# Second layer of a two-layer convolution kernel: two block buffers, a scratch tensor stored row by row, one load for each block

## The chip, the core and the metric

## What is computed

The input x is 8 images of 32 channels of 512 x 512 in float32. Cut to what matters:

```python
# layer 0
x = x + _L0_conv_ref(_gn(x), L0_conv_weight, L0_conv_bias)   # 3x3 convolution of quantised values
# layer 1, on x1 = the x above
v = _gn(x)                                    # groups of 2 channels: (v - mean) / sqrt(var + eps)
feat = einsum('bihw,oi->bohw', v, conv_w) + conv_b
filt = einsum('kh,bchw,lw->bckl', Ph, feat, Pw)   # 5x5 means of feat: a filter for each image and channel
out = x + depthwise 5x5 convolution of feat with filt
```

## The kernel before

Three stages run one after the other: the first layer, a short stage that makes statistics and filter tables, and the second layer.

**First layer** (`quantised_conv`). A chunk is 32 image rows (16 chunks an image). Its SBUF tile `b_x` has row r of each group of 4 in partitions 32r to 32r+31, a channel in each partition, 8 groups side by side; a chunk is loaded by four DMAs of 32 partitions (L321). Part of the next image is streamed through `b_stream` (L355) for its statistics. After the convolution the sum stands in the same tile, and GpSimd stores it to the scratch tensor x1 in HBM (L561), four DMAs of 32 partitions, 2 KB pieces. x1 has the layout image, channel, row, column. SyncE reloads a slot only when its store has landed.

**Second layer** (`depthwise`). An image is 9 blocks of 57 output rows (61 input rows); 72 blocks. Each block goes through 8 steps s, with 4 channels of the output in each step. A group(p, e, j) works on two blocks at once: the pointwise part of block j and the banded part (the 5x5 filter as matmuls with banded tables) of block j-1.

- `c_x` holds one block of x1 in float32, partitions being (column quarter, channel), 61 rows of 128 columns, so rows of 512 B. It has one buffer. Four DMAs load it (L832): SyncE those of quarters 0 and 1, ScalarE those of 2 and 3, both at step 2 of the group before, when VectorE's last c_z of the old block is done (`zl_done`).
- ScalarE writes the high half of a part of the block (a quarter of its columns) to `c_z` (L942), VectorE the low half (L971). Parts 0 and 1 of block j+1 come in steps 6 and 7 of group j, parts 2 and 3 in steps 0 and 1 of the next group.
- TensorE multiplies 8 column positions of `c_z` a step into `c_cps` (24 matmuls, L1032 to L1034). ScalarE takes the result to `c_feat` high (L959), VectorE to `c_feat` low (L997).
- TensorE multiplies the banded tables `c_tt` with `c_feat` into `c_tps` (36 matmuls a step, L1052). Both PSUM tiles have two slots.
- `c_xr` holds x1 for the same output rows, 4 channels a step, 6 slots (half a 128-partition tile each). SyncE loads it (L844): rows 0 to 47 and 48 to 56 in a DMA each, once the slot's old content is stored (`stored`). VectorE adds `c_tps` to it (L1007, two instructions a step), and GpSimd stores it to the output (L911).

SyncE executes one program in order: the c_xr of each step, at step 2 of each group the wait for `zl_done` and its half of c_x, and towards the end of an image the tables. This loop runs from registers (`Fori` over pairs of images). A DMA that stands behind another on the same queue is issued after it.

## Time and profile before

| | us |
|---|---|
| median of 3 runs | 7573.3 (7562.2 to 7585.8) |
| the profiled execution, own time | 7568.0 |
| its span | 7566.2 |
| first layer, about | 0 to 2780 |
| second layer, about | 2930 to 7566 |

The profile is of one execution. Busy time is the time in which an engine ran instructions; matmuls are pipelined, so TensorE's is rough. A wait names the instruction or transfer that came last before the waiting one could go. A wait matters only if the engine that waits, or one that waits for it, sets the pace. Lines such as L1007 are lines of the kernel before. Transfers into SBUF are named by tile: c_x<-x_scratch is a load of the block, c_xr<-x_scratch one of the rows to be added to.

### The profile page before, as it was taken

What the parts mean: (1) busy time and instruction counts of PE and PEld (TensorE: products, weight loads), DVE (VectorE), ACT (ScalarE), POOL (GpSimd) and SP (SyncE); (2) the same over time, 40 slices, a digit from 0 to 9 for tenths busy, and PEclk for the clock granted to TensorE, in tenths of its full rate; (3) what the DMA queues carried; (4) which work ended last, traced back from release to release, by engine and by line L of the source; (5) the groups of instructions that cost most, each with busy time, mean ns of one, the idle gap of its engine ahead of it and who ended that gap; (6) DMA issues with size and microseconds to landing.
All of it is one profiled execution on the core that took longest, in us unless ns stands there. A gap on an engine that the chain in (4) does not pass through costs nothing.

```text
span 7566.2 us, 113303 instructions
## 1 busy us (share of the span) xinstructions
PE 5144.7 (68%) x43798; PEld 3402.5 (45%) x43798; DVE 5236.3 (69%) x5651; ACT 3292.3 (44%) x1645; POOL 995.8 (13%) x1700
## 2 busy tenths in 40 slices
PE   0766666666666753776777776777777677777677
PEld 0111111111111213665666665666666566666566
DVE  4676767777676873666777776766666677677676
ACT  0655546455554743333443343443333343444343
POOL 0011101011010111111111111111111111111111
PEclk9888878877888876888888888888888888888888
DMA  9999999999999866777778778778877877877877
GB/s 199 263 257 285 262 284 261 270 281 272 281 263 290 255 182 137 184 181 193 182 184 198 177 190 197 185 181 204 188 181 187 197 188 177 202 182 179 193 185 184
DMA packets 1136887, 1615.31 MB, mean 213 GB/s; under 512 B 84538, under 2 KB 642874, under 8 KB 1132346
## 3 DMA queue, kind: packets, MB, share of 16 engines
q1 hardware_dynamic: 689154, 928.05, 52.8%
q0 software_dynamic: 166336, 537.04, 24.1%
q10 hardware_dynamic: 280832, 142.62, 8.3%
q8 instruction: 363, 5.95, 0.3%
q14 instruction: 202, 1.65, 0.1%
HBM read 1068.53 MB, written 538.84 MB: 212 GB/s over the span
## 4 chain that ended last, share of the span: by engine, by line
DMA 21%; DVE 14%; PE 9%; issue 8%; SPq 7%; ACT 3%; another core or an unknown queue 1%; POOL 0%; ACTq 0%; DVEq 0%; POOLq 0%
DMA c_x<-x_scratch 12%; DMA c_xr<-x_scratch 9%; PE c_tps L1052 8%; DVE c_z L971 7%; SPq L844 5%; DVE c_xr L1007 5%; DVE c_feat L997 2%; ACT c_z L942 2%; SPq L832 1%; ACT c_feat L959 1%; PE c_cps L1032 0%; PE c_cps L1034 0%; PE c_cps L1033 0%; SPq L849 0%
## 5 line engine op out<-in xcount | busy, mean ns | idle before, releaser
L1052 PE MATMUL c_tps<-c_feat,c_tt 123*128 123x256 f16 (+1 forms) x20736 | 2660.2, 292 | 1183.8 <-DVE c_xr L1007 923.9
L1052 PEld LDWEIGHTS c_tps<-c_feat,c_tt 123*128 123x128 f16 (+1 forms) x20736 | 2130.7, 104 | 1603.3 <-DVE c_xr L1007 878.3
L1007 DVE SCALAR_TENSOR_TENSOR c_xr<-c_tps,c_xr 57x1024 f32<-57x1024 f32 (+1 forms) x1152 | 1403.7, 1218 | 1225.7 <-DMA c_xr<-x_scratch 1114.9
L942 ACT ACTIVATE c_z<-c_x,c_rs 128x1952 f16<-128x1952 f32 x288 | 1062.4, 3690 | 1418.9 <-DMA c_x<-x_scratch 1320.3
L428 PE MATMUL b_ps<-b_xq,w0main 128*128 128x512 bf16 x3072 | 954.1, 416 | 808.5 <-ACT b_q L390 671.5
L959 ACT ACTIVATE c_feat<-c_cps 122x1024 f16<-122x1024 f32 x576 | 818.6, 1423 | 1492.5 <-PE c_cps L1034 1239.0
L911 POOL DMA_DIRECT2D out_dram<-c_xr x1152 | 666.8, 580 | 4040.1 <-DVE c_xr L1007 3962.9
L971 DVE SCALAR_TENSOR_TENSOR c_z<-c_x,c_rs,c_z 128x1952 f16<-128x1952 f32 x288 | 1030.8, 3579 | 195.0 <-ACT c_z L942 192.0
L390 ACT ACTIVATE b_q<-b_ps,q_bias 128x1024 int8<-128x1024 f32 x512 | 549.9, 1113 | 1031.9 <-DVE b_x L506 965.1
L1032 PE MATMUL c_cps<-w_high,c_z 128*128 128x128 f16 x4608 | 813.9, 221 | 190.6 <-DVE c_z L971 122.3
L441 PE MATMUL b_ps<-b_xq,w0edge 64*32 64x512 bf16 x3048 | 926.9, 415 | 0.0
L438 PE MATMUL b_ps<-b_xq,w0edge 64*32 64x512 bf16 x3048 | 925.2, 414 | 0.0
L428 PEld LDWEIGHTS b_ps<-b_xq,w0main 128*128 128x128 bf16 x3072 | 226.0, 101 | 1485.6 <-issue 1232.8
L997 DVE TENSOR_TENSOR c_feat<-c_cps,c_feat 122x1024 f16<-122x1024 f32 x576 | 813.6, 1413 | 71.2 <-ACT c_feat L959 54.0
L465 DVE BATCH_NORM_STATS2 b_stats_x<-b_stream 128x6 f32<-128x512 f32 x672 | 413.9, 680 | 584.4 <-DMA b_stream<-in_x_dram 538.7
L1034 PE MATMUL c_cps<-w_high,c_z 128*128 128x128 f16 x4608 | 812.0, 221 | 0.0
L1033 PE MATMUL c_cps<-w_low,c_z 128*128 128x128 f16 x4608 | 811.7, 220 | 0.0
L517 DVE BATCH_NORM_STATS2 b_stats<-b_x 128x6 f32<-128x408 f32 (+5 forms) x1520 | 645.4, 501 | 4.0
L561 POOL DMA_DIRECT2D x_scratch<-b_x x512 | 298.9, 584 | 2449.6 <-DVE b_cols L521 2248.4
L506 DVE SCALAR_TENSOR_TENSOR b_x<-b_q,b_x 128x2048 f32<-128x2048 int8 x256 | 574.6, 2280 | 60.2 <-ACT b_q L390 60.2
L1032 PEld LDWEIGHTS c_cps<-w_high,c_z 128*128 128x128 f16 x4608 | 454.1, 99 | 203.3 <-DVE c_z L971 116.0
L375 ACT ACTIVATE b_x<-b_x,b_shift,b_scale 128x4096 int8<-128x4096 f32 x128 | 486.7, 3802 | 42.1 <-DVE b_shift L476 40.6
(130 smaller groups left out, 2283.4 us busy)
## 6 DMA issues: line engine op xcount, KB each, us to landing
b_x<-in_x_dram SPq DMA_DIRECT2D x552, 512.0 KB, 15.3
x_scratch<-b_x POOLq DMA_DIRECT2D x512, 512.0 KB, 10.8
c_xr<-x_scratch SPq DMA_DIRECT2D x576, 384.0 KB
out_dram<-c_xr POOLq DMA_DIRECT2D x576, 384.0 KB, 5.1
b_stream<-in_x_dram SPq DMA_DIRECT2D x672, 256.0 KB, 12.9
c_x<-x_scratch SPq DMA_DIRECT2D x112, 976.0 KB, 17.4
c_x<-x_scratch ACTq DMA_DIRECT2D x112, 976.0 KB, 20.9
c_tt<-table_scratch SPq DMA_DIRECT2D x64, 576.0 KB
```

Source lines behind the costliest of these rows:

```text
L428: return pe.matmul(ps[:, g % 3, j, :], k.w0main[:, d, :, :].rearrange("p r o -> p (r o)"), xq[:, n % XQ_SLOTS, 2 * i + j, d:d + W], start= ...
L438: pe.matmul(ps[0:C, g % 3, j, :], k.w0edge[P // 2:P, d, :], xq[P // 2:P, (m - 1) // JB % XQ_SLOTS, (m - 1) % JB, d:d + W], start=False, st ...
L441: pe.matmul(ps[P - C:P, g % 3, j, :], k.w0edge[0:P // 2, d, :], xq[0:P // 2, (m + 1) // JB % XQ_SLOTS, (m + 1) % JB, d:d + W], start=False ...
L942: act.activation(split_part(0, part), positions(part), ACT.Identity, scale=rs[:, :]).then_inc(zh_done, 1)
L959: act.activation(dst, cps[0:MAIN, s % 2, :, :].rearrange("p j (q o) -> p o q j", q=Q), ACT.Identity).then_inc(fh_done, 1)
L971: dve.scalar_tensor_tensor(split_part(1, part), positions(part), rs[:, :], split_part(0, part), ALU.mult, ALU.subtract).then_inc(zl_done, 1)
L997: dve.tensor_tensor(lo, cps[0:MAIN, s % 2, :, :].rearrange("p j (q o) -> p o q j", q=Q), hi, ALU.subtract).then_inc(fl_done, 1)
L1007: last = dve.scalar_tensor_tensor(res, tps[PR * h:PR * h + n, s % 2, :, :], 1.0 / FS, res, ALU.mult, ALU.add)
L1032: pe.matmul(dst, zh, wh, start=True, stop=False)
L1033: pe.matmul(dst, zh, wl, start=False, stop=False)
L1034: last = pe.matmul(dst, zl, wh, start=False, stop=True)
L1052: last = pe.matmul(tps[:, s % 2, o % 4, :], tt[0:rows, o, tp, 2 * d:2 * d + 2, :].rearrange("k w m -> k (w m)"), feat[0:rows, (e * N + i) ...
```

## The change

What it does:

1. x1 is laid out image, row, channel, column. The store from `b_x` is two DMAs of all 128 partitions (4 of the 8 groups each) where it was four of 32. The partitions of `c_x` become (channel, column quarter), and a block is loaded by one DMA over 128 partitions, issued by SyncE; ScalarE issues none. The weight tile `w1_diag` is filled by four small strided loads, and `rstd` is copied to the new partition order (`rstd_cq`).
2. `c_x` gets two buffers. The load of block j+2 is issued at step 5 of group j, when all of block j is split.
3. The parts of a block are split in every second step, two steps ahead of their use; `c_z` holds two parts and no longer a whole block. The order on VectorE is feat, c_z, addition.
4. `c_xr` has 4 slots for 6. Its four channels of a row stand together in HBM, so a row is one run of 8 KB for four of 2 KB.
5. SyncE's program of the second layer is written out for all 72 blocks, with constants for register values.
6. Constants of the first layer are freed before the second, to make room.

The diff, cut to its core:

```diff
-XR_SLOTS = 6
+XR_SLOTS = 4
...
-        x1v = x1.rearrange("b c (n j r) w -> b n r c j w", j=JB, r=4)
+        x1v = x1.rearrange("b (n j r) c w -> b n (r c) j w", j=JB, r=4)
+        STORE = 2 * 16
...
-                    for r in range(Q):
-                        pool.dma_start(x1v[b, n, r, :, :, :], xt[C * r:C * r + C, s, :, :]).then_inc(x1_stored[s], 16)
+                    for h in range(2):
+                        rows = slice(JB // 2 * h, JB // 2 * (h + 1))
+                        pool.dma_start(x1v[b, n, :, rows, :], xt[:, s, rows, :]).then_inc(x1_stored[s], 16)
...
+            for q in range(Q):
+                sp.dma_start(rstd_cq[q::Q, :], rstd[0:C, :]).then_inc(stored, 16)
...
-        xt = sb("c_x", [P, ROWS_IN, P], F32)
-        z = sb("c_z", [P, 2, W // Q // 2, P], F16)
+        xt = sb("c_x", [P, 2, ROWS_IN, P], F32)
+        z = sb("c_z", [P, 2, 2, PAIRS_PART, P], F16)
...
-        x1v = x1.rearrange("b c h (q w) -> b q c h w", q=Q)
+        x1v = x1.rearrange("b h c (q w) -> b (c q) h w", q=Q)
...
-        def load_x1(eng, p, e, j, quarters):
-
-            if (e, j) != (0, 0):
-                eng.wait_ge(zl_done, count(p, e, 4 * N, 4 * j) + START)
+        def load_x1(eng, p, e, j):
+
+            if (e, j) not in ((0, 0), (0, 1)):
+                eng.wait_ge(zl_done, count(p, e, 4 * N, 4 * (j - 1)) + START)
...
-            for q in quarters:
-                eng.dma_start(xt[C * q:C * q + C, lo:hi, :], x1v[e + de::2][p, q, :, r0 + lo:r0 + hi, :]).then_inc(x1_loaded, 16)
+            eng.dma_start(xt[:, x_slot(e, j), lo:hi, :],
+                          x1v[2 * p + e + de, :, r0 + lo:r0 + hi, :]).then_inc(x1_loaded[x_slot(e, j)], 16)
...
-                    if s == 2 and pointwise and (j < N - 1 or another(p, e)):
-                        load_x1(sp, p, e, j + 1, (0, 1))
+                    if s == 5 and pointwise and (j + 2 < N or another(p, e)):
+                        load_x1(sp, p, e, j + 2)
...
-            run(sp, group)
+            group(0, 0, 0, True, False)
+            for p in range(PAIRS):
+                for e in range(2):
+                    for j in range(1, N + 1):
+                        group(p, e, j, p < PAIRS - 1 or e == 0 or j < N, True)
...
-        def convert_order(p, e, j, s):
-
-            if 1 <= j and s < 2:
-                return [(j, 2 + s)]
-            if s >= STEPS - 2 and (j + 1 < N or another(p, e)):
-                return [(j + 1, s - (STEPS - 2))]
-            return []
+        def convert_next(p, e, j, s):
+
+            if s % 2:
+                return None
+            if s < STEPS - 2:
+                return j, s // 2 + 1
+            return (j + 1, 0) if j + 1 < N or another(p, e) else None
...
-                    if s == 2 and (j < N - 1 or another(p, e)):
-                        load_x1(act, p, e, j + 1, (2, 3))
...
-    x1 = nc.dram_tensor("x1_scratch", [nb, C, H, W], F32).ap()
+    x1 = nc.dram_tensor("x1_scratch", [nb, H, C, W], F32).ap()
```

Two places in the program. First SyncE in the middle of a block of the second layer, before: each c_xr is two DMAs (48 and 9 rows), ISA and REGISTER_ALU rows compute addresses, and the two c_x rows are SyncE's half of a block; the c_xr before them is that of step 2.

```order
L844 ISA [waits c_stored4]
L844 DMA c_xr<-x_scratch 48x4x512
L844 ISA
L844 DMA c_xr<-x_scratch 9x4x512
L827 REGISTER_ALU
L832 ISA [waits c_zl_done]
L832 DMA c_x<-x_scratch 32x61x128
L832 ISA
L832 DMA c_x<-x_scratch 32x61x128
L844 ISA [waits c_stored5]
L844 DMA c_xr<-x_scratch 48x4x512
```

The same engine after, in the second group of the image: the c_xr rows shown first are those of steps 4 and 5.

```order
L860 DMA c_xr<-x_scratch 48x2048 [waits c_stored0]
L860 DMA c_xr<-x_scratch 9x2048
L860 DMA c_xr<-x_scratch 48x2048 [waits c_stored1]
L860 DMA c_xr<-x_scratch 9x2048
L847 DMA c_x<-x_scratch 128x61x128 [waits c_zl_done]
L860 DMA c_xr<-x_scratch 48x2048 [waits c_stored2]
L860 DMA c_xr<-x_scratch 9x2048
L860 DMA c_xr<-x_scratch 48x2048 [waits c_stored3]
L860 DMA c_xr<-x_scratch 9x2048
```

The load of the block moved from behind the c_xr of step 2 to behind that of step 5, and it is one DMA of 128 partitions where SyncE had two of 32; the c_xr of steps 6 and 7 stand behind it.

Second VectorE, before, in steps 1 and 2 of a group: c_z is the low half of a part, c_feat the low half of feat, c_xr the addition.

```order
L971 SCALAR_TENSOR_TENSOR c_z<-c_x,c_rs,c_z 128x16x122 [waits c_zh_done]
L994 REGISTER_ALU
L997 TENSOR_TENSOR c_feat<-c_cps,c_feat 122x32x4x8 [waits c_fh_done]
L1007 SCALAR_TENSOR_TENSOR c_xr<-c_tps,c_xr 57x1024 [waits c_xr_loaded3,c_band_done]
L1007 SCALAR_TENSOR_TENSOR c_xr<-c_tps,c_xr 57x1024
L994 REGISTER_ALU
L997 TENSOR_TENSOR c_feat<-c_cps,c_feat 122x32x4x8 [waits c_fh_done]
L1007 SCALAR_TENSOR_TENSOR c_xr<-c_tps,c_xr 57x1024 [waits c_xr_loaded4,c_band_done]
L1007 SCALAR_TENSOR_TENSOR c_xr<-c_tps,c_xr 57x1024
```

And after, one even step and the odd one behind it.

```order
L1016 TENSOR_TENSOR c_feat<-c_cps,c_feat 122x32x4x8 [waits c_fh_done]
L992 REGISTER_ALU
L993 SCALAR_TENSOR_TENSOR c_z<-c_x,c_rs,c_z 128x16x122 [waits c_zh_done]
L1024 REGISTER_ALU
L1029 SCALAR_TENSOR_TENSOR c_xr<-c_tps,c_xr 57x1024 [waits c_xr_loaded2,c_band_done]
L1029 SCALAR_TENSOR_TENSOR c_xr<-c_tps,c_xr 57x1024
L1013 REGISTER_ALU
L1016 TENSOR_TENSOR c_feat<-c_cps,c_feat 122x32x4x8 [waits c_fh_done]
L1024 REGISTER_ALU
L1029 SCALAR_TENSOR_TENSOR c_xr<-c_tps,c_xr 57x1024 [waits c_xr_loaded3,c_band_done]
```

c_z went behind feat, and comes in every second step all through the group where it stood at the head of steps 6, 7, 0 and 1 in a row.

## Rows read from the trace of the kernel before

**Rows 1.** Stretches: length; busy (instructions) by engine; granted clock, DMA share, GB/s

```profile
20.00:170.00 150.00, 0.00 (x0) 0.00 (x0) 72.66 (x120) 0.00 (x0) 0.38 (x1) 1.00 1.07 219
300.00:2700.00 2400.00, 1619.32 (x8437) 418.31 (x8436) 1763.25 (x2994) 1340.14 (x711) 275.48 (x472) 0.82 1.00 274
2930.00:7566.00 4636.00, 3374.84 (x34481) 2936.37 (x34478) 3193.76 (x2032) 1809.41 (x858) 666.83 (x1152) 0.85 0.79 187
```

**Rows 2.** Waits, second layer: us in total, times, longest

```profile
ACT c_z L942 <- DMA c_x<-x_scratch: 1196.8, 70, 23.5
DVE c_xr L1007 <- DMA c_xr<-x_scratch: 1114.9, 78, 18.8
PE c_tps L1052 <- DVE c_xr L1007: 923.9, 91, 15.6
PE c_tps L1052 <- DVE c_feat L997: 259.8, 64, 5.9
...
DVE c_z L971 <- ACT c_z L942: 137.1, 47, 14.2
DVE c_xr L1007 <- PE c_tps L1052: 98.7, 81, 2.0
...
DVE c_feat L997 <- ACT c_feat L959: 54.0, 26, 8.5
```

**Rows 3.** Groups of instructions, second layer: busy us, mean ns, idle before

```profile
L1007 DVE SCALAR_TENSOR_TENSOR c_xr<-c_tps,c_xr 57x1024 f32<-57x1024 f32 (+1 forms) x1152 | 1403.7, 1218 | 1225.7 <-DMA c_xr<-x_scratch 1114.9 <-PE c_tps L1052 98.7
...
L971 DVE SCALAR_TENSOR_TENSOR c_z<-c_x,c_rs,c_z 128x1952 f16<-128x1952 f32 x284 | 1016.7, 3580 | 140.1 <-ACT c_z L942 137.1
...
L997 DVE TENSOR_TENSOR c_feat<-c_cps,c_feat 122x1024 f16<-122x1024 f32 x574 | 810.9, 1413 | 71.2 <-ACT c_feat L959 54.0
```

**Rows 4.** Timeline of SyncE's queue, one block: start us, us, what

```profile
5106.31 1.60 SPq L832 DMA_DIRECT2D c_x<-x_scratch  x2
5108.09 38.33 SPq L844 DMA_DIRECT2D c_xr<-x_scratch  x16
```

**Rows 5.** What SyncE's queue waited for, second layer

```profile
SPq L832 <- DVE c_z L971: 1655.6, 70, 44.0
```

**Rows 6.** The chain that ended last, same block: start us, us, what

```profile
5108.09 9.99 SPq L844
...
5118.26 12.07 DMA c_xr<-x_scratch
```

**Rows 7.** Timeline of VectorE, same block

```profile
5114.29 1.42 DVE L997 TENSOR_TENSOR c_feat<-c_cps,c_feat 122x1024 f16<-122x1024 f32 x1
5130.43 1.22 DVE L1007 SCALAR_TENSOR_TENSOR c_xr<-c_tps,c_xr 57x1024 f32<-57x1024 f32 x1 [14.71 <-DMA c_xr<-x_scratch]
```

**Rows 8.** Timeline of TensorE, the banded matmuls of three steps after a wait

```profile
5006.46 6.29 PE L1052 MATMUL c_tps<-c_feat,c_tt 123*128 123x256 f16 x36 [12.61 <-DVE c_xr L1007]
...
5013.93 4.11 PE L1052 MATMUL c_tps<-c_feat,c_tt 123*128 123x256 f16 x36
...
5019.22 4.11 PE L1052 MATMUL c_tps<-c_feat,c_tt 123*128 123x256 f16 x36
```

**Rows 9.** DMA queues, 5108 to 5110: packets, MB, share of 16 engines

```profile
q1 hardware_dynamic: 589, 0.30, 72.0%
q10 hardware_dynamic: 30, 0.02, 3.4%
```

**Rows 10.** DMA queues, 2866 to 2870

```profile
q1 hardware_dynamic: 1140, 0.58, 58.3%
q10 hardware_dynamic: 1142, 0.58, 57.5%
```

**Rows 11.** DMA queues, 5117 to 5121

```profile
q0 software_dynamic: 254, 0.67, 42.4%
```

**Rows 12.** DMA queues, 300 to 2700

```profile
q1 hardware_dynamic: 217601, 409.80, 68.9%
q0 software_dynamic: 67408, 245.46, 30.7%
```

**Rows 13.** The output stores of L911, from its own view

```profile
DMA to landing us min/median/max: 2.8/5.7/18.9
```

**Rows 14.** What SyncE's queue waited for, first layer

```profile
SPq L321 <- DMA x_scratch<-b_x: 701.7, 96, 23.0
```

**Rows 15.** Timeline of ScalarE, first block of the second layer

```profile
2855.57 2.55 ACTq L832 DMA_DIRECT2D c_x<-x_scratch  x2
2907.32 3.57 ACT L942 ACTIVATE c_z<-c_x,c_rs 128x1952 f16<-128x1952 f32 x1 [123.59 <-DMA c_x<-x_scratch]
```

More of the change, by code:

```diff
@@ L45 @@
 SPLIT = 48
+PAIRS_PART = 16
 def edges(i):
@@ L600, in _, with filters @@
             dve.wait_ge(kept, 1 + START)
-def filters(nc, nb, k, sums, mean, rstd, table_d, bias_d):
+def filters(nc, nb, k, sums, mean, rstd, rstd_cq, table_d, bias_d):
     lots = -(-nb // 4)
@@ L731, in _ @@
         def _(sp):
+            for q in range(Q):
+                sp.dma_start(rstd_cq[q::Q, :], rstd[0:C, :]).then_inc(stored, 16)
             sp.wait_ge(tables_ready, 1)
@@ L762, in depthwise @@
         xr = sb("c_xr", [P, XR_SLOTS // 2, 4, W], F32)
-        rs = sb("c_rs", [P, 1], F32)
+        rs = sb("c_rs", [P, 2], F32)
         cps = ctx.enter_context(nc.psum_tensor("c_cps", [P, 2, 8, P], F32))
         tps = ctx.enter_context(nc.psum_tensor("c_tps", [P, 2, 4, HW2], F32))
-        x1_loaded, edge_loaded = sem("c_x1_loaded"), sem("c_edge_loaded")
+        x1_loaded = [sem(f"c_x1_loaded{i}") for i in range(2)]
+        edge_loaded = sem("c_edge_loaded")
         t_loaded = [sem(f"c_t_loaded{i}") for i in range(4)]
@@ L947, in group @@
                 if not banded:
-                    load_x1(act, p, e, 0, (2, 3))
-                    for part in range(4):
-                        high(p, e, 0, part)
+                    high(p, e, 0, 0)
                 else:
@@ L954, in group @@
                 for s in range(STEPS):
-                    for blk, part in convert_order(p, e, j, s):
-                        high(p, e, blk, part)
+                    nxt = convert_next(p, e, j, s)
+                    if nxt is not None:
+                        high(p, e, *nxt)
                     act.wait_ge(conv_done, count(p, e, TILES, STEPS * j + s + 1) + START)
@@ L998, in group @@
                                           ALU.subtract).then_inc(fl_done, 1)
+                        nxt = convert_next(p, e, j, s)
+                        if nxt is not None:
+                            low(p, e, *nxt)
                     if banded:
@@ L1011, in _ @@
             for t in range(2):
-                dve.memset(z[:, t, :, MAIN:P], 0.0).then_inc(started, 1)
+                dve.memset(z[:, t, :, :, MAIN:P], 0.0).then_inc(started, 1)
             for slot in range(2):
@@ L1029, in pointwise @@
                 for c in range(8):
-                    zh, zl = (z[:, t, 8 * s + c, :] for t in range(2))
+                    zh, zl = (z[:, s // 2 % 2, t, 8 * (s % 2) + c, :] for t in range(2))
                     dst = cps[:, s % 2, c, :]
@@ L1087, in conv_preact_2 @@
-        k.b1col = sb("b1col", [P, 1], F32)
-        k.below = sb("below", [P, NBINS - 1], F32)
-        k.above = sb("above", [P, NBINS - 1], F32)
-        k.bin_weight = sb("bin_weight", [P, NBINS, NBINS], F32)
-        own = sb("own", [P, nb, 2], F32)
-        mean = sb("mean", [P, nb], F32)
-        rstd = sb("rstd", [P, nb], F32)
-        with ExitStack() as tmp:
-            weights_and_masks(nc, tmp, k, w0, b0, w1, b1)
-        with nc.sbuf_tensor("sums", [P, nb, NSEG, 2 * NBINS - 1], F32) as sums:
-            quantised_conv(nc, nb, k, x, x1, own, sums)
-            statistics_of_x1(nc, nb, k, own, mean, rstd)
-            filters(nc, nb, k, sums, mean, rstd, table_d, bias_d)
@@ L1100, in conv_preact_2, with early @@
-        depthwise(nc, nb, k, x1, rstd, table_d, bias_d, out)
+        rstd_cq = sb("rstd_cq", [P, nb], F32)
+        with ExitStack() as first:
+            def early(name, shape, dt):
+                return first.enter_context(nc.sbuf_tensor(name, shape, dt))
+            k.same_group = early("same_group", [P, P], F32)
+            k.same_channel = early("same_channel", [P, P], F32)
+            k.w0main = early("w0main", [P, 3, Q, C], BF16)
+            k.w0edge = early("w0edge", [P, 3, C], BF16)
+            k.w1t = early("w1t", [P, C], F32)
+            k.wf = early("w1_diag", [P, Q, C], F32)
+            k.b0col = early("b0col", [P, 1], F32)
+            k.q_bias = early("q_bias", [P, 1], F32)
+            k.b1col = early("b1col", [P, 1], F32)
+            k.below = early("below", [P, NBINS - 1], F32)
+            k.above = early("above", [P, NBINS - 1], F32)
+            k.bin_weight = early("bin_weight", [P, NBINS, NBINS], F32)
+            own = early("own", [P, nb, 2], F32)
+            mean = early("mean", [P, nb], F32)
+            rstd = early("rstd", [P, nb], F32)
+            with ExitStack() as tmp:
+                weights_and_masks(nc, tmp, k, w0, b0, w1, b1)
+            with nc.sbuf_tensor("sums", [P, nb, NSEG, 2 * NBINS - 1], F32) as sums:
+                quantised_conv(nc, nb, k, x, x1, own, sums)
+                statistics_of_x1(nc, nb, k, own, mean, rstd)
+                filters(nc, nb, k, sums, mean, rstd, rstd_cq, table_d, bias_d)
@@ L1104 @@
+        depthwise(nc, nb, k, x1, rstd_cq, table_d, bias_d, out)
 _INS = ["x", "L0_conv_weight", "L0_conv_bias", "L1_conv_conv_w", "L1_conv_conv_b"]
```

75 lines of the change are left out of this document (37 added, 38 removed).

## The prediction

> **What bounds the kernel now.** I read the stretches first [rows 1]. The first layer (300 to 2700 us) keeps the DMA engines busy all the time, share 1.00 at 274 GB/s; the second (2930 to 7566, 4636 us) does not, 0.79 at 187 GB/s. The reader is to see there that no engine is full (VectorE 3193.8 us, TensorE 3374.8), so a wait sets the pace. The table of waits says which [rows 2]: VectorE's addition L1007 waits 1114.9 us for the transfers c_xr, 78 times, some 14 us each; for ScalarE's c_z it waits 137.1, for ScalarE's feat 54.0, for TensorE 98.7, while TensorE waits 923.9 and 259.8 for VectorE. ScalarE waits longer for the blocks c_x (1196.8) but has room for it. The second layer is 72 blocks (8 images of 9), so a block takes 4636/72 = 64.4 us. VectorE's work in it, from the mean durations [rows 3]: 16 x 1.218 + 4 x 3.580 + 8 x 1.413 = 45.1 us. The rest is 15.5 of c_xr waits and 3.8 of others.
>
> **Where the c_xr wait is born.** Three engines in one block: SyncE sends its half of c_x at 5106.31, and only then the c_xr of step 3 [rows 4]; it had sat waiting for VectorE's c_z (L832, 1655.6 us in all) though slots were free [rows 5]. The chain shows SyncE held for 9.99 us in that next issue, then 12.07 us to its landing [rows 6]; VectorE had finished feat of step 3 by 5115.7 and goes on at 5130.43 [rows 7]. From the issue of c_x to the addition behind it are L = 24.1 us. Work that VectorE has in hand at that point: two additions and three feats, 9.1 us. So the wait is about 15: that is the pace. The block is L plus the work from that addition to the c_z that releases the next c_x: 2.44 + 2 x 3.85 + 3 x 7.43 + 3.58 = 36.0 (3.85 a step without c_z, 7.43 with one), plus 3.8 of small waits: 63.9, against 64.4 seen.
>
> **The change, part by part.** *SyncE's order.* By the order of the program c_x of block j+2 stands behind the c_xr of step 5, and steps 6 and 7 and the following ones stand behind it. Its wait is for the last c_z of block j, now in step 4. So the loop has the old shape: c_x issued at the end of c_z in step 4, c_xr of step 6 behind it on the same queue. Work in hand: additions of 4 and 5, feats of 5 and 6, c_z of 6, 2.44 x 2 + 1.41 x 2 + 3.58 = 11.3 us. Work after: addition 6 (2.44), steps 7, 1, 3 (11.6), steps 0 and 2 (14.9), feat and c_z of step 4 (5.0), together 33.9. Block time T = L' + 33.9 + small waits. Four slots instead of six matter little for step 7 to step 1 (their slots are free by then); later slots are asked for again after some 7.5 us (POOL's issue 0.6, landing 5 to 6 [rows 13]) of about 20 us of work.
>
> *What the earlier load buys.* c_x is needed a block after its issue, so ScalarE's 1196.8 us of waiting goes, but VectorE had only 137.1/72 = 1.9 us a block of it, and ScalarE no longer issues DMAs (0.75 a block of feat waits). A c_z in every second step evens VectorE's pairs of steps at 11.3 us against TensorE's 2 x 5.3 (from one group of 36 matmuls to the next 5.29); after a stop that group takes 6.29 where it takes 4.11 in full run [rows 8]. I leave 2.1 us of small waits where 3.8 were, bounds 1 and 4. T = L' + 36.0.
>
> *L', the term that decides.* Before, two queues carried the block: 3904 packets of 512 B on SyncE's, 3904 on ScalarE's. Now all 7808 (128 partitions x 61 rows) are on SyncE's. While SyncE's queue was nearly alone it started 589 packets in 2 us, 295 in a us, and its packets took 72% of the engines, so the engines had time left [rows 9]. With both queues in flight, each started 1140 in 4 us, 285 in a us, and the engines were full [rows 10]. A queue alone thus is no faster than a queue beside another. One point speaks for more than 295: SyncE's packets took 0.72 x 32/589 us = 39 ns alone, 33 beside ScalarE's; with the gap of 15 ns kept and 33 ns of packet it would be 333. I take 320, bounds 240 (64 KB from row to row of a partition may be worse than 2 KB) and 592 (both queues' engine limit, 27 ns). So 7808/320 = 24.4 us; out's packets, those of three steps, some 340 of 4 KB at 166 ns [rows 11], take 3.5 us of the engines, of which 3.0 hold it up, the rest falls into its gaps; first packet 1.4 after the issue; then c_xr of step 6 at 8 KB a row: 467 KB at the 219 GB/s of loads that go to half the partitions [rows 1] is 2.1, landing and wake-up 1.5. L' = 32.4, T = 68.4, or 4.0 more than 64.4. Over the 70 blocks that have such a load: +280 us. The place: T = 44.0 + 7808/R, and every 10% of R is about 2.4 us a block, 170 us in all.
>
> The row says one queue gives half of two. The Trainium skill, "DMA: Bandwidth & Descriptors", section "Issuing engines are not separate DMA queues", says that all queues run on the same 16 engines and that a second issuer saves sequencer time only. By that rule R would be that of both queues, 570, and T 57.7; by the row it is about 300. It is the rival C below.
>
> *The store of x1.* Four stores of 32 partitions become two of 128, and a row's 32 channels stand together. The stores took 30.7% of 2400 us for 245.46 MB in 4 KB packets, 197 ns each [rows 12]; where stores ran among loads they took 166 ns (42.4% of 4 us, 0.67 MB) [rows 11]. Loads alone into 32 partitions at a time make 219 GB/s with full engines [rows 1], so a transfer over part of the partitions is slowed by its own kind. If all 65,536 packets fall to 166: 65536 x 31 ns/16 = 127 us, and since the layer's engines are full it would be time won. I take 100, bounds 150 won and 60 lost (SyncE waits 701.7 us for these stores [rows 14], and a slot now needs both of two bigger ones).
>
> On this the skill speaks for the change: "SBUF — State Buffer", section "Door 1: The DMA port swizzle (why `[64,N]` ≈ `[32,N]`)", gives 32 partitions 8 of 16 ports, some 218 GB/s; the 219 GB/s of the load-only stretch agrees.
>
> *At nothing, or nearly.* c_xr at 8 KB a row: 3.65 MB a block in a quarter of the pieces, on a queue that then is idle; only the one behind c_x is in the sum. w1 by four tiny loads and rstd by four, 2 to 3 us once. SyncE's written-out program drops its register steps (37 and 29 ns each), none on the path for more than 0.1 us a block, and adds code to fetch. First block: c_x 0 and 1 now stand before the tables on the queue, about 50 us for both, where before 51.7 us went by from the issue to the first c_z [rows 15]; within 15 us either way.
>
> **The sum**, on the profiled execution's own 7568 us (the median of three is 7573, 5 more): 7568 + 280 - 100 = 7748, say 7750.
>
> **Rivals.**
> A, the forecast: one queue starts 265 to 353 packets a us; T 73.5 to 66.1; 8105 down to 7590.
> B, slower still: the new rows of 64 KB slow each read. R under 265, for instance 240: T 76.5, 7568 + 847 - 100 = 8315. Against it: a block's 64 KB rows are read whole by neighbouring partitions.
> C, faster than before: a single load over all 128 partitions runs at what both queues did. The wait of L1029 then shrinks, since T falls below 64.4 at R above 383, with the store's 100 us counted above 358. At 412: T 63.0, 7370; at 500: 59.6, 7130; at 592: 57.2, 6965. For it: 39 against 33 ns, and engines not full in [rows 9]. Against it: 285 a us beside another queue, where the packets were short too.
> D, the stall doesn't occur: c_xr of step 6 gets past c_x. Then VectorE's 45.1 and 2 of small waits bind, unless the DMA engines do, 0.79 x 64.4 = 50.9 us of work now; 7568 - 70 x 13.5 - 100 = 6523. Against it: [rows 6], where nothing passed.
> E, no change: R of 353 to 363, within 0.3% (what a measurement of this kernel can tell from nothing).
>
> **Chances.** A 0.42, B 0.13, C 0.36, D 0.03, E 0.06. Slower by over 0.3%: A and B, 0.55; within 0.3% 0.06; faster 0.39. The range leaves out the ends of C with D (below 7150, some 0.11) and of B (above 8250, 0.08). The likeliest case's own range is 7590 to 8105. The sign is nearly open: it hangs on one rate.
>
> **What would show it.** c_x<-x1_scratch of L847 landing 26 to 30 us after its issue (C: under 22, B: over 33); VectorE's L1029 waiting for c_xr once a block for some 20 us, 1400 to 1500 us in all (C: under 1000); ScalarE's wait for c_x gone; q10 empty; the first layer shorter by 100 us, with q0's share of it near 26%. Wrong at once if the c_xr of step 6 lands before the c_x ahead of it, if another engine than VectorE fills the block, or if the first layer grows.

## The result, and the profile after

The changed kernel takes 7232.0 us (median of 4 runs, 7227.2 to 7241.2), the kernel before 7571.1 beside it: ratio 0.9552, interval 0.9534 to 0.9570. The forecast was 7750, slower; it is 339 us faster. The profiled execution has a span of 7229.0 us against 7566.2.

Stretches of the kernel after, to be held against [rows 1] (length; busy time and instructions of TensorE, its weight loads, VectorE, ScalarE, GpSimd; granted clock, DMA share, GB/s):

```profile
20.00:170.00 150.00, 0.00 (x0) 0.00 (x0) 67.81 (x112) 0.00 (x0) 1.11 (x3) 1.00 1.06 209
300.00:2700.00 2400.00, 1607.63 (x8372) 423.70 (x8528) 1778.80 (x3018) 1355.90 (x720) 178.09 (x238) 0.82 1.01 276
2900.00:7229.00 4329.00, 3205.95 (x34346) 2854.01 (x34343) 3184.40 (x2025) 1821.20 (x850) 666.77 (x1152) 0.87 0.80 199
```

The first layer is as full and as fast as it was, with one difference that nobody forecast: in the stretch of loads alone it makes 209 GB/s where it made 219, although these loads are unchanged and no store runs yet. The second is shorter with the same work in it, and its engines are no fuller in share. The waits, against [rows 2]:

```profile
DVE c_xr L1029 <- DMA c_xr<-x_scratch: 1043.2, 80, 20.6
...
PE c_tps L1074 <- DVE c_feat L1016: 859.7, 63, 15.6
```

VectorE still waits for c_xr about once a block. TensorE's wait now shows under feat: the feat of the next step stands behind the addition that stalls (it runs from 5021.61 to 5023.00 in the block below, and TensorE's matmuls start at 5023.24). ScalarE's 1196.8 us for c_x are gone; what it waits for c_x now is 87.1 us, once, before the first block, where that was 123.59 [rows 15]. One block, as SyncE and the chain show it (start us, us, what), against [rows 4] and [rows 6]:

```profile
4995.69 0.70 SPq L847
...
4996.43 14.89 SPq L860
...
5011.37 7.66 DMA c_xr<-x_scratch
...
5019.12 0.10 DVE c_xr L1029
```

and VectorE in the same block, against [rows 7]:

```profile
5003.24 3.61 DVE L993 SCALAR_TENSOR_TENSOR c_z<-c_x,c_rs,c_z 128x1952 f16<-128x1952 f32 x1
5019.12 2.46 DVE L1029 SCALAR_TENSOR_TENSOR c_xr<-c_tps,c_xr 57x1024 f32<-57x1024 f32 x2 [12.28 <-DMA c_xr<-x_scratch]
```

The reader is to see the old stall in its new place: the block's load goes out at 4995.69, SyncE is held for 14.89 us in the issue of c_xr behind it, and VectorE runs dry at 5006.84 and goes on at 5019.12. From issue to addition are 23.4 us. The load itself lands sooner than forecast, in its view:

```profile
L847 SPq DMA_DIRECT2D c_x<-x_scratch x72: 700/701/10860, 2837.9 to 7067.1; - x72
...
DMA to landing us min/median/max: 16.0/21.8/32.8
```

From the issue at 2888.31 (the third block's) to the last are 69 blocks: 60.56 us each, where it was 64.4. Where the 337 us of span went: 70 x 3.84 = 269; the first block waits 16.1 us from issue to first c_z (2837.92 to 2854.02) where it was 51.7 [rows 15], 36; the first layer ends (its last statistics on ScalarE) at 2766.73 instead of 2783.52, 17; the remaining 15 lie in the rest of the ends.

Of the 3.84 us that a block gained, only 0.7 are from the load: issue to addition went from 24.1 to 23.4. The others lie outside it, 64.4 - 24.1 = 40.3 before and 60.56 - 23.4 = 37.1 now: some 2 because more of VectorE's work stands ahead of the stalled addition (11.3 us for 9.1), some 1 because the small waits are shorter. The single queue did not beat the two; it only lost nothing against them.

### The profile page after: what moved, and what is told of

Same layout as the page of the kernel before. It is cut to its first block, busy times and chain, and to the rows that moved or that the text cites. A ratio compares the mean times of both kernels' runs of the same rounds, so it can differ in the third digit from the quotient of the medians.

```text
span 7229.0 us, 109542 instructions
## 1 busy us (share of the span) xinstructions
PE 4958.3 (69%) x43630; PEld 3334.5 (46%) x43798; DVE 5237.7 (72%) x5646; ACT 3317.4 (46%) x1645; POOL 887.5 (12%) x1442
## 2 busy tenths in 40 slices
DMA packets 617506, 1615.13 MB, mean 223 GB/s; under 512 B 81274, under 2 KB 82554, under 8 KB 580218
## 3 DMA queue, kind: packets, MB, share of 16 engines
q0 software_dynamic: 162176, 537.03, 24.4%
## 4 chain that ended last, share of the span: by engine, by line
SPq 15%; DVE 14%; DMA 12%; PE 10%; issue 7%; ACT 1%; POOL 0%; DVEq 0%; POOLq 0%; ACTq 0%
SPq L860 14%; DMA c_xr<-x_scratch 10%; PE c_tps L1074 8%; DVE c_z L993 5%; DVE c_xr L1029 5%; DVE c_feat L1016 4%; DMA out_dram<-c_xr 2%; ACT c_feat L983 1%; PE c_cps L1056 1%; PE c_cps L1054 1%; PE c_cps L1055 1%; SPq L847 1%; SPq L875 0%; DMA c_x<-x_scratch 0%; POOL c_feat L918 0%
## 5 line engine op out<-in xcount | busy, mean ns | idle before, releaser
L1074 PE MATMUL c_tps<-c_feat,c_tt 123*128 123x256 f16 (+1 forms) x20736 | 2521.9, 283 | 1096.1 <-DVE c_feat L1016 859.7
L1074 PEld LDWEIGHTS c_tps<-c_feat,c_tt 123*128 123x128 f16 (+1 forms) x20736 | 2064.3, 101 | 1434.0 <-DVE c_feat L1016 783.0
L1029 DVE SCALAR_TENSOR_TENSOR c_xr<-c_tps,c_xr 57x1024 f32<-57x1024 f32 (+1 forms) x1152 | 1406.2, 1221 | 1084.5 <-DMA c_xr<-x_scratch 1043.2
L433 PE MATMUL b_ps<-b_xq,w0main 128*128 128x512 bf16 x2904 | 910.7, 416 | 819.4 <-ACT b_q L395 654.3
L567 POOL DMA_DIRECT2D x_scratch<-b_x x256 | 191.6, 753 | 2541.9 <-DVE b_cols L526 2527.4
```

What stands on the lines that cost most here:

```text
L433: return pe.matmul(ps[:, g % 3, j, :], k.w0main[:, d, :, :].rearrange("p r o -> p (r o)"), xq[:, n % XQ_SLOTS, 2 * i + j, d:d + W], start= ...
L1029: last = dve.scalar_tensor_tensor(res, tps[PR * h:PR * h + n, s % 2, :, :], 1.0 / FS, res, ALU.mult, ALU.add)
L1074: last = pe.matmul(tps[:, s % 2, o % 4, :], tt[0:rows, o, tp, 2 * d:2 * d + 2, :].rearrange("k w m -> k (w m)"), feat[0:rows, (e * N + i) ...
```

## Experiments: what sets the rate of a load

The question is why one queue did in some 13 to 14 us (13.6 by the rate of a_gap below) what the forecast gave it 24 for. Theories: **source runs**, partitions that are neighbours now read neighbouring 512 B, so that packets merge; **one DMA** in place of four; **partition range**, a DMA over 128 partitions can write twice as fast as one over 32 or 64 neighbours; **written-out program**, SyncE issues without register steps. And whether the stall is an order in one queue or something that any queue would suffer.

**Source runs (a_gap).** The load of a block with its partitions 1 KB apart in HBM; it reads other data of the same size.

```diff
-            eng.dma_start(xt[:, x_slot(e, j), lo:hi, :],
-                          x1v[2 * p + e + de, :, r0 + lo:r0 + hi, :]).then_inc(x1_loaded[x_slot(e, j)], 16)
+            r1 = r0 + lo - (r0 + hi == H)
+            src = x1[2 * p + e + de, r1:r1 + hi - lo, :, :]
+            src = bass.AP(tensor=src.tensor, offset=src.offset, ap=[[2 * P, P], [C * W, hi - lo], [1, P]])
+            eng.dma_start(xt[:, x_slot(e, j), lo:hi, :], src).then_inc(x1_loaded[x_slot(e, j)], 16)
```

> The changed kernel with one edit: the load of a block is still one DMA over 128 partitions of 61 rows of 512 B from rows 64 KB apart, but neighbouring partitions read from places 1 KB apart in HBM instead of 512 B, so that no two of them adjoin (the values are other ones, the output is not the reference's). Theory S (the length of the source's contiguous run sets the packets: 2 KB over four partitions, and larger packets let one queue fill the engines): packets of 512 B again, one queue at some 290 a us, the block lands 28 to 32 us after its issue instead of 21.8, a block takes 68 to 72 us, 7232 + 70 x 9 = about 7860. Theory O (a single load over all 128 partitions and 16 engines' own partitions is what made it fast): packets may be short, but landing stays at 22 us and the time at 7232.

7233.1 us, 0.9566 (0.9549 to 0.9583): no change. Packets under 2 KB went from 82554 to 639610, so they had merged, four runs to a 2 KB packet, and it is worth nothing. The two kernels' queues in 2 us with only the block's load in flight (packets, MB, share of 16 engines), first 5068 to 5070 of the kernel after (293 GB/s in all), then 5069 to 5071 of a_gap (303):

```profile
q1 hardware_dynamic: 286, 0.59, 100.4%
```

```profile
q1 hardware_dynamic: 1151, 0.59, 113.8%
```

One queue alone starts 575 packets of 512 B a us. The forecast took 320.

**Four and two DMAs over neighbours (a_four, a_two).** The changed kernel with its block load in four DMAs of 32 partitions, or two of 64; the same queue.

```diff
-            eng.dma_start(xt[:, x_slot(e, j), lo:hi, :],
-                          x1v[2 * p + e + de, :, r0 + lo:r0 + hi, :]).then_inc(x1_loaded[x_slot(e, j)], 16)
+            for k in range(Q):
+                eng.dma_start(xt[C * k:C * k + C, x_slot(e, j), lo:hi, :],
+                              x1v[2 * p + e + de, C * k:C * k + C, r0 + lo:r0 + hi, :]).then_inc(x1_loaded[x_slot(e, j)], 16)
```

> The changed kernel with the load of a block cut into four DMAs of 32 partitions each on SyncE's queue; four neighbouring partitions still read one 2 KB run. Theory S: packets stay 2 KB, and the time stays within 2% of 7232 (7232 to 7400; a little slower if 32 partitions at a time hold it to the 209 to 219 GB/s of the first layer's loads, 4.0 MB in 18.5 us where 20 are seen). Theory O: the rate of the kernel before comes back, a block 68 us or more, 7800.

> The changed kernel with the load of a block cut into two DMAs of 64 neighbouring partitions each on SyncE's queue. 
a_four 7716.9 us, 1.0211 (1.0194 to 1.0229); a_two 7724.7, 1.0208 (1.0189 to 1.0226). Both lose all of the gain and more, and two DMAs lose as much as four, so it isn't their number. (That four DMAs need not be slow, b_oneq_stride shows below, at 590 packets a us in its best 2 us.) With the cut the packets of the load are of 512 B again (643067 and 640762 under 2 KB in the two runs, about as many as in a_gap), though neighbouring partitions still read neighbouring bytes; why they don't merge stays open. So a_gap, whose packets are of 512 B too, is the run to hold them against, and it leaves the partition range and the number of DMAs as the difference. Waiting for c_xr is 1502.1 and 1523.9 us. a_four, 5050 to 5052, its block's load alone in flight:

```profile
q1 hardware_dynamic: 685, 0.34, 121.5%
```

a_two makes 339 a us in 5062 to 5064. In a_four it is 342 packets a us at full engines: 47 ns each where a_gap has 28 (32 us of engine time over 685 and 1151). With R = 342 the forecast's own line T = 44.0 + 7808/R gives 66.8; a_four's measured 7717 is 485 us over the kernel after, 6.9 a block, so 67.5.

**Which partitions two queues write at one time (b_same_half).** The kernel before, where SyncE wrote partitions 0 to 63 while ScalarE wrote 64 to 127. Only the quarters are dealt out otherwise (and so other columns of x1 are in flight together).

```diff
-                        load_x1(sp, p, e, j + 1, (0, 1))
+                        load_x1(sp, p, e, j + 1, (0, 2))
...
-                        load_x1(act, p, e, j + 1, (2, 3))
+                        load_x1(act, p, e, j + 1, (1, 3))
```

> The kernel before (7571 us) with nothing changed but which engine issues which quarter of a block: SyncE quarters 0 and 2, ScalarE quarters 1 and 3, where it was 0 and 1, and 2 and 3. Queues, number of DMAs, packets, bytes and waits stay. Before, SyncE wrote partitions 0 to 63 while ScalarE wrote 64 to 127; now both write 0 to 63 and then both 64 to 127. Partition-range theory: the two queues together make the 342 packets a us that one queue made into neighbouring partitions, 22.8 us a block where it was 13.7, so about what one queue gave (8026): 7900 to 8060. Theory that a second queue is what adds rate: 7571 within 0.3%, 7548 to 7594.

7891.5 us, 1.0426 (1.0406 to 1.0445): 320 us for another order of the same quarters; a little under the lower end expected. Both queues in the first block, 2893 to 2897, 14 to 18 us after its issue:

```profile
q10 hardware_dynamic: 690, 0.35, 61.5%
q1 hardware_dynamic: 690, 0.35, 61.1%
```

1380 packets in 4 us from two queues; in [rows 10], with the halves apart, 2282. The two windows are not at the same place in their loads: [rows 10] lies 10 to 14 us behind the issue. At that place b_same_half makes 1862 (2889.83 to 2893.83); 7 to 11 us behind the issue it makes 1463 (2886.83 to 2890.83) where the kernel before makes 2411 (2863 to 2867). So it is 345 to 366 packets a us on either side of a short burst. The burst comes about where each queue should pass to its second load; that the two then write different halves for a moment would fit, but the trace doesn't show it. The rate went by the half of the partitions that was written, not by the number of queues; a_stride below, which changes the destination alone, says the same.

**All four loads on one queue (b_oneq), and then spread (b_oneq_stride).** The kernel before with ScalarE's two loads moved to SyncE; then the same with load q into every fourth partition (for the time only: the numbers it computes are other ones).

```diff
-                        load_x1(sp, p, e, j + 1, (0, 1))
+                        load_x1(sp, p, e, j + 1, (0, 1, 2, 3))
...
-                    if s == 2 and (j < N - 1 or another(p, e)):
-                        load_x1(act, p, e, j + 1, (2, 3))
...
-                eng.dma_start(xt[C * q:C * q + C, lo:hi, :], x1v[e + de::2][p, q, :, r0 + lo:r0 + hi, :]).then_inc(x1_loaded, 16)
+                eng.dma_start(xt[q::Q, lo:hi, :], x1v[e + de::2][p, q, :, r0 + lo:r0 + hi, :]).then_inc(x1_loaded, 16)
```

> The kernel before with all four c_x DMAs of a block on SyncE's queue. This is the term of the prediction by itself: one queue, rows of 512 B, 32 partitions at a time. The prediction's rate of 295 to 320 packets a us makes 24.4 to 26.5 us for a block, so c_xr of step 3 lands some 8 to 11 us later after the issue than 24.1, less what ScalarE gets back: 7560 + 70 x 7 to 9 = 8050 to 8200. Theory H gives the same: 52 ns a packet, 7808 x 52/16 = 25.4 us. Rival (a queue alone isn't held by anything, the engines are shared anyhow): within 1% of the kernel before.

> The kernel before with all four loads of a block on SyncE's queue (8026 us as measured with neighbouring partitions), and one thing more: load q goes to partitions q, q+4, q+8, ... instead of 32q to 32q+31. The bytes, the runs of 512 B in HBM, the number of DMAs and the queue stay; the numbers computed in the second layer are then not the kernel's, only the time is read. Partition-range theory (a DMA over 32 or 64 neighbouring partitions gets half of the SBUF side): the 7808 packets of a block go from 46 ns to about 31 ns, 22.4 us to 15.1 us a block, 7.3 us over 71 blocks: 7450 to 7570 us, so no slower than the kernel before with its two queues. Theory that one DMA for the block is what helped, or that four DMAs on a queue run one after the other: 8000 to 8050, as with neighbouring partitions.

b_oneq 8026.0 us, 1.0604 (1.0583 to 1.0625), just under the 8050 expected; b_oneq_stride 7743.2, 1.0228 (1.0204 to 1.0252). Spreading gives 283 us back, against both rival theories, but 450 to 580 were expected. In b_oneq_stride the rate isn't even within a block: 798 packets in 2 us at 5051, 1180 at 5054. Its slow part is the start of the load. Two kernels with one queue and all 128 partitions, both in their first block from 1 to 5 us behind the issue, first b_oneq_stride (2859.6 to 2863.6), then a_gap (2832 to 2836):

```profile
q1 hardware_dynamic: 1035, 0.53, 60.1%
```

```profile
q1 hardware_dynamic: 2124, 1.09, 98.4%
```

The slow start goes with the kernel before: that kernel makes 1225 packets at this place (2856.57 to 2860.57), b_same_half 1220, b_oneq 1020, whichever partitions they write, while a_gap starts at full rate and a_four, into 32 partitions, makes 824 in its first 2 us (2841.7 to 2843.7). Between the two groups lie the layout of x1 in HBM, the order of c_x's partitions and its second buffer, and for a_gap also one DMA in place of four; no run changes one of them alone, so what holds the start back stays open. It matters for the forecast, since [rows 9] lies in such a start, 2 to 4 us behind the issue at 5106.31.

**The written-out program (a_four_loop).** a_four with SyncE's second layer as a loop again.

```diff
-            for p in range(PAIRS):
-                for e in range(2):
-                    for j in range(1, N + 1):
-                        group(p, e, j, p < PAIRS - 1 or e == 0 or j < N, True)
+            run(sp, group)
```

> The changed kernel with four loads of 32 neighbouring partitions a block on SyncE (7717 us as measured with SyncE's program written out), and SyncE's program as a loop over pairs of images, as in the kernel before. If the written-out program is worth nothing on the path: 7717 within 0.3%, 7694 to 7740. If a register step of 30 to 40 ns ahead of each issue counts (32 issues a block): up to 1 us a block more, 7740 to 7790. If fetching the written-out code costs time: 7650 to 7694.

7714.3 us, 1.0183 (1.0161 to 1.0205), beside 7716.9: nothing, as forecast.

**Another queue (a_actq).** ScalarE issues the block loads from the third on, after its c_feat of step 5 (its program is written out for that, as SyncE's is). Now c_xr doesn't stand behind c_x.

```diff
-                    if s == 5 and pointwise and (j + 2 < N or another(p, e)):
-                        load_x1(sp, p, e, j + 2)
...
+                    if s == 5 and (j + 2 < N or another(p, e)):
+                        load_x1(act, p, e, j + 2)
```

> The changed kernel with the loads of all blocks but the first two issued by ScalarE at step 5 (its program written out), so that the c_xr of step 6 no longer stands behind the block on SyncE's queue. Theory F (the order on one queue makes VectorE wait): VectorE's 1043 us of waiting for c_xr fall under 300, a block takes 48 to 53 us, 6350 to 6700 in all, and the next bound is the DMA engines (share 0.80 of 60.5 us = 48 us a block) or VectorE's 45.1 us. Rival (the DMA engines' traffic itself delays c_xr, whatever the queue): the wait stays above 800 us and the time within 2% of 7232.

6524.3 us, 0.8633 (0.8616 to 0.8649), 708 less than the kernel after; the wait is a little above the 300 us expected. The wait and the stretch of the second layer:

```profile
DVE c_xr L1033 <- DMA c_xr<-x_scratch: 344.5, 124, 34.1
```

```profile
2900.00:6500.00 3600.00, 3144.34 (x34332) 2808.78 (x34330) 3191.46 (x2025) 1835.11 (x926) 664.54 (x1144) 0.95 0.96 240
```

The DMA engines are 0.96 busy where they were 0.80: two thirds of the stall are gone. That the transfers bind next is likely from that share, not tested. This is what the prediction's rival D put at 6523, by another way: the c_xr doesn't pass c_x in its queue, it has a queue of its own. D's bound by the DMA engines was 50.9 us a block, and a_actq's block is 50.28 (69 blocks from 2905.2 to 6374.4). That the totals agree to 1 us is luck: D also counts 100 us for the store, of which 17 came.

**Pieces (a_pieces).** The block's load in four DMAs of a quarter of the rows each over 128 partitions, on SyncE behind the c_xr of steps 5, 6, 7 and 0.

```diff
+            for k in pieces:
+                a, z = lo + (hi - lo) * k // 4, lo + (hi - lo) * (k + 1) // 4
+                eng.dma_start(xt[:, x_slot(e, j), a:z, :],
+                              x1v[2 * p + e + de, :, r0 + a:r0 + z, :]).then_inc(x1_loaded[x_slot(e, j)], 16)
...
-                    if s == 5 and pointwise and (j + 2 < N or another(p, e)):
-                        load_x1(sp, p, e, j + 2)
+                    if s >= 5 and pointwise and (j + 2 < N or another(p, e)):
+                        load_x1(sp, p, e, j + 2, (s - 5,))
+                    if s == 0 and banded and pointwise and (j + 1 < N or another(p, e)):
+                        load_x1(sp, p, e, j + 1, (3,))
```

> The changed kernel with the load of a block cut by rows into four DMAs of about 15 rows over 128 partitions, issued behind the c_xr of steps 5, 6, 7 and 0. Theory F: each c_xr has a quarter of a block ahead of it, some 5 us, against 11.3 us of work in hand; the wait for c_xr falls under 300 us, 6350 to 6700 in all. Rival (traffic, not order): above 800 us of wait and 7100 or more. If both this and the issue by ScalarE fall short of 6700 the DMA engines bind.

6880.8 us, 0.9107 (0.9083 to 0.9132). VectorE's wait for c_xr is 696.8 us in 159 pieces, 4.4 us each twice a block, where it was 13 once. Half of what the second queue gives, and short of the 6350 to 6700 expected, which took each piece to hide wholly.

**The first layer.** The store in four DMAs of 32 partitions as before, the layout kept (a_store4); its loads into every fourth partition, store as changed (a_stride, for the time only, as its numbers are other ones). a_store4's store is the loop of the kernel before; a_stride's edit, made for `b_stream` too:

```diff
-                sp.dma_start(xt[C * r:C * r + C, s, :, :], xv[b, n, r, :, :, :]).then_inc(x_loaded[s], 16)
+                sp.dma_start(xt[r::Q, s, :, :], xv[b, n, r, :, :, :]).then_inc(x_loaded[s], 16)
```

> The changed kernel with the store of the first layer as four DMAs of 32 partitions again (x1 row by row as in the change). If the store over 128 partitions made the first layer's 17 us: 7232 + 17 = 7249, packets of 4 KB at 196 ns instead of 168. If the layout did: 7232.

> The changed kernel with each of the first layer's loads (b_x and b_stream) written to every fourth partition from r on (r, r+4, ... r+124) instead of 32 neighbouring ones; the same bytes, sizes and queue, but the rows then stand in the wrong partitions and the output is not the reference's. Theory H: 32 partitions spread over all ports, so the load-only stretch rises from 209 GB/s to 300 or more, the 2 KB packets fall from 141 ns to 90 to 100, and the first layer ends 400 to 600 us earlier (2767 to 2200 to 2370), 6650 to 6830 in all. Theory N (32 partitions make small DMAs, whichever they are): the first layer stays at 2767 us, 7232 in all.

a_store4 7230.0 us, 0.9553 (0.9540 to 0.9566): the store's width is worth nothing. a_stride 6701.3, 0.8847 (0.8834 to 0.8861), its first layer ending at 2235.78 instead of 2766.73. The loads alone, 60 to 100 us, first in the kernel after, then in a_stride:

```profile
60.00:100.00 40.00, 0.00 (x0) 0.00 (x0) 19.38 (x32) 0.00 (x0) 0.00 (x0) 1.00 1.06 208
```

```profile
60.00:100.00 40.00, 0.00 (x0) 0.00 (x0) 35.75 (x60) 0.00 (x0) 0.00 (x0) 1.00 1.05 387
```

At the same busy share a packet takes 84 ns for 158 (1.051 x 640 us over 8023 packets, 1.063 x 640 over 4315). With the stores, 300 to 2200 us, it is 333 GB/s at a share of 0.90 where the kernel after has 275 at 1.01. So the first layer was bound by writing 32 neighbouring partitions at a time.

**The two gains together (a_act_stride, a_act_first, a_act_two).** First the spread loads on top of a_actq, for the time only; then two ways that keep the kernel's numbers: the loads cut by group of rows over all 128 partitions, or b_x's upper half issued by ScalarE.

> Two edits that were measured apart, together: blocks issued by ScalarE (6524 us against 7232) and the first layer's loads to every fourth partition (6701 against 7232, all of it in the first layer; the numbers computed are not the kernel's, only the time is read). If the two stages are independent, as the theory has it: 6524 - 531 = 5993, range 5960 to 6030. If the second layer's gain rested on something the first layer leaves behind (DMA engines or clock): 6050 or more.

> The kernel with blocks issued by ScalarE (6524 us), and its first layer's loads cut another way: not by row of the group of four (32 partitions a DMA), but by group: each DMA carries one group of four rows over all 128 partitions, 2 KB packets as before, 8 DMAs a chunk instead of 4, and 4 for each half of the streamed part. Partition-range theory: the loads reach what the loads to every fourth partition reached, so the first layer ends near 2240 us and the whole near 5983 us; with twice the issues on SyncE 5950 to 6080. If the gain of the loads to every fourth partition came from something else (the order in which channels are read, or that only each fourth partition is written): 6400 to 6550, no better than 6524. If more and smaller DMAs cost what the wider ones gain: 6100 to 6400.

> The kernel with blocks issued by ScalarE (6524 us), and in its first layer the loads of b_x shared out: SyncE those into partitions 0 to 63, ScalarE those into 64 to 127, issued at the end of each of its chunks; the streamed part stays with SyncE. Partition-range theory: while ScalarE's loads write the upper half, SyncE's b_x loads write the lower, and the stretch of the first layer that is bound by its loads gets shorter; SyncE keeps about 70% of the load bytes, so the layer ends between 2250 and 2550 us where it was 2783, the whole 6000 to 6300. If only the engines' own limit mattered: no change, 6500 to 6550. If ScalarE's waits for the stores of x1 hold its convolution work up: above 6550.

a_act_first:

```diff
-            for r in range(Q):
-                sp.dma_start(xt[C * r:C * r + C, s, :, :], xv[b, n, r, :, :, :]).then_inc(x_loaded[s], 16)
+            for k in range(JB):
+                sp.dma_start(xt[:, s, k, :], xv[b, n, :, :, k, :]).then_inc(x_loaded[s], 16)
```

a_act_two:

```diff
-                load_chunk(sp, xv, 0, n)
+                load_chunk(sp, xv, 0, n, (0, 1))
...
                         round_out(b, n - 2, 3)
+                        m = n + X_SLOTS - 4
+                        if AHEAD <= m < N:
+                            act.wait_ge(x1_stored[m % X_SLOTS], (b * (2 * STORE) + (STORE if m >= X_SLOTS else 0)) + 16)
+                            load_chunk(act, xv, b, m, (2, 3))
```

a_act_stride 5982.8 us, 0.7905 (0.7889 to 0.7920): the stages add, 5993 was expected. a_act_first 9110.0, 1.2038 (1.2009 to 1.2068), far outside every expectation. Its loads, 100 to 102 us, 101 GB/s:

```profile
q1 hardware_dynamic: 103, 0.20, 26.4%
```

A packet takes 0.264 x 32/103 us = 82 ns, as short as the 84 ns of a_stride, but only a quarter of the engines is at work. The outermost dimension of such a DMA is the 4 rows of a group; the share speaks for one engine for each of them. No other run varies that dimension, so the cause is likely, not shown.

a_act_two 6303.2 us, 0.8323 (0.8308 to 0.8339), the fastest version that computes the same as both kernels. Its first layer ends at 2550.76, and both that and the whole lie just past the far end of what was expected (2550 and 6300). With two queues on opposite halves its loads alone make 365 GB/s in 60 to 100 us, where one queue on one half makes 208; with the stores, 300 to 2400, it is 293.

## Why the prediction was wrong, step by step

- **What bounds the kernel, and where the wait is born**: right. The stall came where the order of the program put it, behind the c_x of step 5, once a block. a_actq shows that it is that order: with c_x on another queue the kernel is 708 us faster.
- **T = L' + 36.0**: right in kind, a little low. 60.56 - 23.4 leaves 37.1.
- **L' = 32.4, the term that failed**; it is 23.4. The failed step is "A queue alone thus is no faster than a queue beside another." [rows 9] and [rows 10] were read as a limit of the queue. In [rows 9] SyncE's queue was writing into one half of the partitions; in [rows 10] the two queues wrote into different halves. 32 us of engine time over 589 packets is 54 ns each, not far from a_four's 47, and 64 us over 2282 packets 28 ns, that of a_gap. "The engines had time left" rested on a share of 72%; a_four shows 121.5% for traffic of the same kind at 342 packets, so this share doesn't say how many more could be started. ([rows 9] had a second thing against it: it lies in the slow start of a load, which a_gap and a_four, with the new layout, don't show; its cause is open.) The change removes the condition under which the rate was read: it writes all 128 partitions in one DMA. 7808 packets at 575 a us take 13.6 us, not 24.4. By T = 44.0 + 7808/R that is T = 57.6, 3 us below the measured 60.56; that much, the rest of L' (9.8 us, not 8.0) and of the small waits (3.2, not 2.1) were short.
- **Why it could be known.** [rows 1] had it: loads alone into 32 partitions made 219 GB/s with engines at 1.07, and the prediction said that such a transfer "is slowed by its own kind", for the store. The same sentence holds for c_x of before, whose DMAs covered 32 partitions. Rival C, with 0.36, named the right outcome for the queue, a single load over all 128 partitions at the rate of both queues. That the measured 7232 lies between its 7370 and 7130 is luck: with R = 575 its sum gives 7568 - 70 x 6.8 - 100 = 6992. Its T is 3 us too low (some 210 in all), 83 us of the store didn't come, and 36 us of the first block and 15 of the ends came unforeseen.
- The Trainium skill, "SBUF — State Buffer", section "Door 1: The DMA port swizzle (why `[64,N]` ≈ `[32,N]`)", states that 32 partitions, and 0 to 63 as well, reach 8 of 16 ports. a_four and a_two (7717 and 7725), b_same_half (7891 against 7571) and a_stride (387 against 208 GB/s) agree; b_oneq_stride (7743) does in part. The prediction cited it for the store only.
- The Trainium skill, "DMA: Bandwidth & Descriptors", section "Issuing engines are not separate DMA queues", by which one queue should do what two did, agrees with a_gap's 575 a us. The section also says that a second issuer saves only the time to initiate a DMA, usually small. Here that time is not small for what stands behind a load: SyncE is held 14.89 us in the issue of c_xr, and a_actq is 708 us faster.
- **The store, -100 us**: 17 came. Its first half was right: q0 made 249.61 MB of 4 KB packets in 26.7% of 2400 us, 168 ns each where 166 were forecast. But the loads beside it took it back. The rows, 300 to 2700, against [rows 12]:

```profile
q1 hardware_dynamic: 218629, 411.72, 73.5%
q0 software_dynamic: 64753, 249.61, 26.7%
```

  SyncE's packets rose from 0.689 x 38400/217601 us = 122 ns to 129. The prediction added the store's time up as if freed engine time were free; the loads into a quarter of the partitions were the limit (a_stride). a_store4 against the kernel after shows the exchange by itself: store packets of 184 ns where they are 168, SyncE's of 125 where they are 129, and the first layer ends no later (2755.9 and 2766.7). That is about half of the rise. The other half, before against a_store4, need not be the store's at all: where loads run alone and no store does, 20 to 170 us, their packets also went from 150 to 157 ns (160 in a_store4), which is the 209 GB/s for 219 of above. Why unchanged loads are slower in the new kernel is not shown.
- **First block, "within 15 us either way"**: it gained 36.
- **At nothing**: right for the written-out program (a_four_loop). ScalarE's wait is gone and q10 is empty, as said. Landing: 21.8 us at the median, which the prediction had named as the mark of C; L1029's 1043.2 us lie just above C's mark of 1000.
- The forecast's own arithmetic, with 342 for 320, is right to 1 us a block for another kernel than the one forecast: a_four.

## To carry to other kernels

Before a rate of a DMA queue goes into a sum, look at which SBUF partitions the measured transfers wrote at that time, and which the new ones will write; a load over all 128, or two queues in opposite halves, made 570 packets of 512 B a us where 32 or 64 neighbours made 340. Look also whether the rate was read at the start of a transfer or in its middle. Then look at what stands behind a large load on its queue: a small transfer that the pace depends on belongs on another queue than the large one. Where the engines are full, time saved on one kind of packet is only won if that kind was the limit.

## What the runs showed of the hardware that was not expected

- One queue makes 575 packets of 512 B a us (a_gap), as many as two queues in [rows 10], 570.
- The same bytes in packets of 2 KB or 512 B into 128 partitions: 7232 and 7233 us. 293 and 303 GB/s.
- Two queues whose loads write the same half of the partitions together make 345 to 366 packets a us (b_same_half) but for a short burst, hardly more than one queue, 342 (a_four).
- 32 partitions spread over all 128 are fast in the first layer (387 GB/s) but only in part in the second (b_oneq_stride, 399 to 590 packets a us).
- In the kernel before and its variants the first block's load starts slowly, 255 to 306 packets a us from 1 to 5 us behind its issue, whatever partitions and queues it uses; in a_gap, with the changed layout and one DMA, it is 531. The cause is open.
- A block's load cut by partitions (a_four, a_two) falls back from packets of 2 KB to 512 B. Open.
- The first layer's unchanged loads alone make 209 GB/s after where they made 219 before. Open.
- A load whose outermost dimension is 4 kept 26.4% of 16 engines busy and made 101 GB/s (a_act_first).
